# An expert and attention layer whose scattering and gathering DMAs lose their limit of two in flight

## What is computed

```python
xn = layernorm(x)
# attention over channels, for each batch
q, k, v = xn @ Wq, xn @ Wk, xn @ Wv
s = swap(softmax(swap(q) @ k / sqrt(8)) @ swap(v)) @ Wo
# experts
scores = softmax(xn @ gate.T)          # 32 experts in 8 groups, the best 3 groups stay
weight, idx = top_k(masked scores, 6); weight /= sum(weight)
y = sum over the 6 of weight * ((silu(xn @ w1.T) * (xn @ w3.T)) @ w2.T)
shared = (silu(xn @ sw1.T) * (xn @ sw3.T)) @ sw2.T
out = x + s * silu(y + shared)
```

## Time and profile before

| | |
|---|---|
| three runs, us | 965.66, 969.05, 969.32; median 969.05 |
| the profiled execution, us | 964.12 |
| its span, first to last instruction | 962.4 |
| busy: PE, PEld | 596.8, 486.4 (62%, 51%) |
| busy: DVE, ACT, POOL | 506.7, 341.5, 399.2 (53%, 35%, 41%) |
| DMA | 174.75 MB, mean 182 GB/s |
| mean granted clock of TensorE | 0.804 of full speed |

### The profile page before, as it was taken

One profiled execution on the slowest core, in us unless ns is written; L12 is line 12 of the kernel. 1 busy time (PEld: TensorE's weight loads), 2 busy tenths in 40 slices (PEclk: granted clock), 3 DMA queues, 4 the chain that ended last, 5 costly groups with the idle time before them and its releaser, 6 DMA issues.

```text
span 962.4 us, 13698 instructions
## 1 busy us (share of the span) xinstructions
PE 596.8 (62%) x3728; PEld 486.4 (51%) x3728; DVE 506.7 (53%) x1412; ACT 341.5 (35%) x684; POOL 399.2 (41%) x401
## 2 busy tenths in 40 slices
PE   5788782928375776001979776758486765658540
PEld 4567551817164654001968665546375654547430
DVE  7877863736374771000535555546465645646543
ACT  3343431332323242001646443435254443435330
POOL 0135345455364663663001444343444444453443
PEclk9798795867768686655979797879799897979875
DMA  9994572634524223224437675758677675848552
GB/s 335 390 356 164 182 262 93 234 132 140 210 73 141 76 93 132 82 82 136 145 120 218 192 237 171 219 154 251 176 220 224 189 208 168 241 148 259 164 170 76
DMA packets 134232, 174.75 MB, mean 182 GB/s; under 512 B 12433, under 2 KB 120722, under 8 KB 133266
## 3 DMA queue, kind: packets, MB, share of 16 engines
q1 hardware_dynamic: 109698, 107.77, 34.3%
q0 software_dynamic: 18432, 50.36, 17.4%
q10 hardware_dynamic: 6032, 15.76, 4.7%
HBM read 81.56 MB, written 92.28 MB: 181 GB/s over the span
## 4 chain that ended last, share of the span: by engine, by line
DMA 57%; issue 21%; POOL 9%; PE 8%; DVE 4%; POOLq 1%; ACT 0%; SPq 0%; DVEq 0%; ACTq 0%
DMA early<-slots_d,slot_at 30%; DMA slots_d<-early,slot_at 23%; POOL slots_d L391 7%; PE ps L696 4%; DMA slots_d<-pad 3%; DVE ps L957 3%; POOL early L408 2%; PE ps L715 2%; PE ps L684 1%; PE ps L706 1%; DVE work L974 1%; POOLq L391 0%; SPq L290 0%; DMA work<-slots_d 0%; DMA slots_d<-early 0%
## 5 line engine op out<-in xcount | busy, mean ns | idle before, releaser
L408 POOL DMA_INDIRECT early<-slots_d,slot_at x192 | 191.7, 999 | 316.9 <-DVE ps L957 108.2
L391 POOL DMA_INDIRECT slots_d<-early,slot_at x192 | 205.4, 1070 | 237.8 <-DMA slots_d<-early,slot_at 170.5
L696 PE MATMUL ps<-w_all,work 128*128 x1344 | 186.5, 294 | 57.3 <-issue 54.2
L696 PEld LDWEIGHTS ps<-w_all,work 128*128 128x128 f16 x1344 | 140.5, 105 | 83.1 <-issue 60.4
L684 PE MATMUL ps<-ident,work 128*128 128x128 f32 x448 | 75.2, 294 | 140.1 <-DMA work<-slots_d 65.9
L957 DVE SCALAR_TENSOR_TENSOR ps<-early,wk,ps 128x256 f32<-128x256 f32 x160 | 77.8, 486 | 116.9 <-DMA early<-slots_d,slot_at 115.5
L684 PEld LDWEIGHTS ps<-ident,work 128*128 128x128 f32 x448 | 54.7, 151 | 155.7 <-issue 81.4
L974 DVE SCALAR_TENSOR_TENSOR work<-ps,work 128x512 f16<-128x512 f32 x112 | 76.8, 686 | 103.6 <-ACT work L517 102.1
L517 ACT ACTIVATE work<-ps 128x512 f16<-128x512 f32 x112 | 66.6, 595 | 141.0 <-PE ps L684 128.1
L715 PE MATMUL ps<-w_all,work 128*128 x672 | 99.9, 289 | 2.5 <-DVE work L987 2.0
L524 ACT ACTIVATE work<-ps 128x256 f32<-128x256 f32 x112 | 43.0, 384 | 157.1 <-PE ps L696 127.4
(11 more groups left out here) (140 smaller groups left out, 811.6 us busy)
## 6 DMA issues: line engine op xcount, KB each, us to landing
work<-slots_d SPq DMA_DIRECT2D x112, 256.0 KB
slots_d<-early SPq DMA_DIRECT2D x112, 256.0 KB
slots_d<-pad SPq DMA_DIRECT2D x7, 3072.0 KB, 15.5
w_all<-in_wexp ACTq DMA_DIRECT2D x7, 1536.0 KB, 6.9
slots_d<-pad SPq DMA_DIRECT2D x1, 7168.0 KB, 30.0
s_all<-in_x SPq DMA_DIRECT2D x8, 512.0 KB, 4.8
ysh_d<-work ACTq DMA_DIRECT2D x8, 512.0 KB
early<-ysh_d SPq DMA_DIRECT2D x32, 128.0 KB
```

The costliest lines, as they stand in the source:

```text
L391: pool.indirect_dma_start(slots_d[:, :], bass.IndirectOffsetOnAxis(ap=slot_at[:, at:at + 1], axis=0), xn[b % XN_RING][:, t, :], None, boun ...
L408: pool.indirect_dma_start(gath[:, at % RING, :], None, slots_d[:, :], bass.IndirectOffsetOnAxis(ap=slot_at[:, at:at + 1], axis=0), bounds_ ...
L696: mm = pe.matmul(ps[:, 2 + p % 2, h * 2 * I:(h + 1) * 2 * I], xT[p % 2][:, x_low, h, k, :], w16[:, bass.ds(at_weights[2 * p + h] + w_low * ...
```

## The change

The constant `FLIGHT = 2` goes, and with it the two waits of GpSimd for the indirect DMA two before (L390 and L407 of the kernel before). The two semaphores `s_disp`, to which the scatters posted in turn, become three sets of twelve, one set for each place in the ring of normalized rows; of a batch's 24 scatters two post to each. Whoever waits for a batch's scatters waits for the twelve semaphores of its set to reach the count of that batch: VectorE in `normal`, SyncE before the last weights and before the first pair of slots.

```diff
-FLIGHT = 2
+COUNTS = 12
@@
-        s_disp = sems("s_disp", FLIGHT)
+        s_disp = [sems(f"s_disp{r}_", COUNTS) for r in range(XN_RING)]
@@ sync
-            for f in range(FLIGHT):
-                sp.wait_ge(s_disp[f], 16 * (BATCH_ROWS // FLIGHT) * (B - 2))
+            for landed in s_disp[2]:
+                sp.wait_ge(landed, 16 * (BATCH_ROWS // COUNTS) * 2)
@@
-            for f in range(FLIGHT):
-                sp.wait_ge(s_disp[f], 16 * (BATCH_ROWS // FLIGHT) * B)
+            for k, n in enumerate((3, 3, 2)):
+                for landed in s_disp[k]:
+                    sp.wait_ge(landed, 16 * (BATCH_ROWS // COUNTS) * n)
@@ gpsimd, scatters
-                        if at >= FLIGHT:
-                            pool.wait_ge(s_disp[at % FLIGHT], 16 * (at // FLIGHT))
                         pool.indirect_dma_start(slots_d[:, :], bass.IndirectOffsetOnAxis(ap=slot_at[:, at:at + 1], axis=0),
                                                 xn[b % XN_RING][:, t, :], None, bounds_check=SLOTS - 1,
-                                                oob_is_err=False).then_inc(s_disp[at % FLIGHT], 16)
+                                                oob_is_err=False).then_inc(s_disp[b % XN_RING][at % COUNTS], 16)
@@ gpsimd, gathers
-                    if at >= FLIGHT:
-                        pool.wait_ge(s_gath[(at - FLIGHT) % RING], 16 * ((at - FLIGHT) // RING) + 16)
@@ vector, normal
-                    for f in range(FLIGHT):
-                        dve.wait_ge(s_disp[f], 16 * (BATCH_ROWS // FLIGHT) * (b - XN_RING + 1))
+                    for landed in s_disp[b % XN_RING]:
+                        dve.wait_ge(landed, 16 * (BATCH_ROWS // COUNTS) * (b // XN_RING))
```

## The result

| | before | changed |
|---|---|---|
| median, us | 967.99 (965.66 to 969.32) | 895.61 (890.39 to 903.28) |
| profiled execution, span | 964.12, 962.4 | 896.77, 895.0 |
| first scatter, first gather, end of span | 35.5, 523.1, 962.4 | 35.5, 458.0, 895.0 |
| mean granted clock | 0.804 | 0.843 |

The ratio is 0.9261 (95% interval 0.919 to 0.9332): faster, as forecast, but 895.6 us instead of 761, outside the range of 728 to 846. Measured again, the same kernel took 760.2 us in one sitting and 893.8 us in another; a large part of this text is about that difference. A sitting is one series of runs on one chip, with the kernel before run in between. The executions of a kernel in one sitting lie close together: here from 890.4 to 903.3 us, in the sitting with 760.2 us within 0.3 us.

What follows compares the result with a forecast made beforehand. Two trains of 192 indirect DMAs issued by GpSimd, two in flight, were taken as the bound. Span 413.9 + 308 + 16.8 + 18.2 = 756.9 us, 758.6 with 1.7 around it, plus 3 of profile shift: 761; range 728 to 846.

Steps and rivals of the forecast that it cites:

- A scatter at 1.28 us, 33.4 us for 24: Stage 1: without waits a scatter costs 0.97 + 0.31 us; a batch's 24, with one stretched by VectorE, take 33.4 us.
- L853 of batch 7 at 289.3: Stage 1: VectorE's write of batch 7's first slots moves from 348.6 to 289.3 us as 59.3 us of waits go.
- (4): Semaphore waits of VectorE and SyncE: 17 ns per bare wait, VectorE's 0.9 us hidden, taken as 0.5 us inside the rounding.
- Pair 24 at 413.9: Stage 2 up to pair 24 moves as a block: pair 24 starts at 413.9 us instead of 535.35.
- Seven cycles of 44.0: Stage 2, pairs 24 to 108: twelve pairs take 44.0 us, from 42.1, slower steps and a microsecond of sums; seven make 308.
- The end: Stage 2 after pair 108: 16.8 us to the last store, then 18.2 us to the end instead of 33.5.
- Rival A, throughput: Both stages: long scatters are throughput, not latency; stage 1 gains 62 us instead of 121.5, span 841; chance 0.15.
- B: Indirect DMA queue: it takes no third DMA, so GpSimd waits inside the instruction; 964 us, no change; chance 0.04.
- C: Indirect DMA queue: past a few flights GpSimd hands over one DMA at a time; slower, about 1310 us; chance 0.03.
- D, the port lock against VectorE: Stage 1: GpSimd's hold on the shared port locks out VectorE; slower, losing from 14 us a batch; chance 0.02.
- (1): Stage 1: GpSimd's waits for earlier indirect DMAs go, VectorE becomes the bound; ends at 326.0 instead of 447.5, 121.5 us less.
- (2): Stage 2: steps of 2.71 us, twelve pairs in 44.0, seven times 308 us, 67 less; shorter end; span 756.9 us.

Runs made afterwards that it cites:

- sitting 2: Changed kernel rerun unaltered on another chip, kernel before 962.9 us: 760.2 us, ratio 0.7887; with two semaphores for each ring place instead of twelve, 750.7 us.
- Sitting 6: Against the changed kernel: scatters bare with a 128x512 fill behind each gather, 781.3 us; two semaphores for each ring place, 752.5 us; kernel before 963.1 us.
- the kernel with the doubled fill: Changed kernel with scatters bare and a GpSimd fill of 128x512 behind each gather: 781.3 us.
- The filled kernel with the wider gap: Changed kernel with a GpSimd fill of 128x256 behind each scatter and 128x512 behind each gather: 788.8 us.

## Why the prediction was right, and where it was wrong

It holds for a sitting with prompt updates (760.2 us) and is 135 us short of the first measurement. Point by point, first on sitting 2:

- **A scatter at 1.28 us, 33.4 us for 24.** Right: issues from 219.39 to 251.48 are 32.1 us, plus 1.28. VectorE's 59.3 us of waits for scatters before L755 are gone; the 2.8 us that are left before it (L752 now) have VectorE's own instruction before as releaser.
- **L853 of batch 7 at 289.3.** It was 295.07, with the last scatter at 330.2 instead of some 323. The step that failed is (4): the semaphores, taken at 0.5 us inside the rounding. With two semaphores instead of twelve, in the same sitting, the last batch's L850 comes at 286.77, 8.3 us earlier, and the whole is 9.5 us shorter. Sitting 6 repeats it: 287.29 with two, 295.11 with twelve (the kernel with the doubled fill, whose stage 1 is the same). I had priced VectorE's ten more waits in each of five batches at SyncE's 17 ns. 2.5 us of the 8.3 stand as idle time before L752 (2.8 against 0.3), 4.6 before L814 (30.4 against 25.8), in a chain that goes once round VectorE, TensorE and back; why the latter grows isn't settled, and that the waits themselves are the cost is thus argued, not shown.
- **Pair 24 at 413.9.** 421.38, 7.5 us late. **Seven cycles of 44.0.** 43.0: (722.21 - 421.38) / 7, so 7.2 us less than I took; my three terms (42.1, 0.6 and 1) add up to 43.7 only, so that 2 of the 7.2 us are a slip in the sum. **The end.** 36.2 us behind pair 108 instead of 35.0. The sum of these three errors, 7.5 - 7.2 + 1.2, is +1.5 us of span: 758.4 against 756.9. Two errors of 7 us cancel, so that the nearness of 760.2 to 761 is in part luck.

The timeline of sitting 2, with batch 7's L850 and pairs 24 and 108:

```profile
295.07 0.18 DVE L850 TENSOR_SCALAR slot_at<-top 128x24 int32<-128x24 f32 x1
...
421.38 2.74 PE L693 MATMUL ps<-w_all,work 128*128 x12 [7.74 <-issue]
...
722.21 2.74 PE L693 MATMUL ps<-w_all,work 128*128 x12 [3.60 <-issue]
```

and batch 7's L850 with two semaphores:

```profile
286.77 0.18 DVE L850 TENSOR_SCALAR slot_at<-top 128x24 int32<-128x24 f32 x1
```

- **Rival A, throughput.** Fell. In the 30 us from 36 to 66, with pads and weights beside them, 24 scatters are issued instead of 10, and the DMA engines move 392 GB/s instead of the 377 of the earlier trace rows:

```profile
36.00:66.00 30.00, 26.57 (x114) 20.87 (x114) 22.51 (x87) 8.07 (x18) 22.98 (x24) 0.84 1.08 392
```

- **B and C, the queue takes no third.** Fell in every sitting: the median scatter takes 972 to 976 ns of GpSimd. (What the prediction quotes against B is about the writing of descriptors, not about how many DMAs a queue takes; the runs alone settle it.) **D, the port lock against VectorE.** Fell: VectorE is busy for 508.8 us in sitting 2 and 511.1 in the first measurement, 506.7 before. The page "SBUF — State Buffer" of the Trainium skill, section "SBUF: two separate sides", adds that TensorE and ScalarE wait on nobody's port; TensorE's matmuls do start on time here, and of its semaphore updates the section says nothing.

On the first measurement the failed step is in (1) and (2) alike: that VectorE's cadence of 37.7 us and the 2.71 us steps are kept when GpSimd issues more densely. Both hang on TensorE's semaphore updates arriving at once. The views of the before-trace show no late one, and I took that to hold for trains without a pause; its records had the sign, 17 late updates behind pairs of gathers. I had weighed GpSimd's effect on VectorE (D) and on the queue (A to C) and none on TensorE. The cost by place: 48.8 us at the first gather (458.0 against 409.2) and 437.0 - 349.2 = 87.8 us behind it, together the 136.6 us between the two spans. The cadence of stage 1 is 44.4 us instead of 37.7, the cycle of twelve pairs 54.8 instead of 44.0. The rivals held 24% of the chance and none had this mechanism, so the range stopped 50 us short.

**Shown:** it is TensorE's updates that are late; they come with the sitting and not with the code alone, since the same kernel has them in two sittings and not in a third; where a sitting has them, they need GpSimd to issue indirect DMAs close behind each other; spacing the scatters by 0.2 us more ends them in stage 1 (1.46 us a scatter), spacing the gathers by 0.4 us more in stage 2 (1.71 us a gather; 1.49 is not enough); neither twelve semaphores nor more than four in flight are needed. **Open:** what makes a sitting have them, the recording of the profile not excluded, by which path GpSimd's issuing holds back TensorE's updates, and whether the pause or the other work of GpSimd in it is what helps (in stage 1 of the kernel before, idle pauses of 0.9 us behind every second scatter went with none late). The filled kernel with the wider gap (788.8 us where prompt) was not run with late updates; my estimate from its two stages, 414.9 + 371.8, is some 787 us of span there, about 107 us less than the changed kernel, for 29 us more where updates are prompt.

## What to carry to other kernels

Taking a depth limit off GpSimd's indirect DMAs pays what the waits show, if everything else on the path stays as prompt; a limit also spaces the issues, and this spacing can be what keeps another engine's semaphore updates prompt. If late updates show, space such issues by a little GpSimd work of the kernel's own where they would run bare beside a chain of TensorE results, and measure in more than one sitting before a time is called the kernel's. Count the trace's semaphore records as well: here every sitting with late updates had lost a part of them. Post to few semaphores: with ten more waits in each of five batches the last batch's slots came 8.3 us later here.

## What the hardware showed

- TensorE's semaphore updates arrived up to some 10 us after its matmuls (236.95 to 246.57), in their order and 0.04 to 0.1 us apart, 2.3 us behind the end of a train of GpSimd's indirect DMAs; one passed earlier, during the train (at 238.12). VectorE's chain of dependent instructions ran through the same train without a gap, to 236.9 us, while L601 of TensorE, ended at 235.23, released ScalarE at 238.14 only. One kernel, two times 135 us apart (760.2 and 895.6), each within 1.5% in its sitting.
- GpSimd hands over an indirect DMA every 1.28 us with no limit in flight, beside full DMA engines (share 1.08).
- A wait of GpSimd for a landing already past costs nothing beside the 0.30 us between two of its DMAs.
